# Response phase of a two-block image kernel: the last eleven strips of the second product rotate over three pairs of PSUM banks, the output and residual rings grow by one, and the scale is placed ahead of the add

## The reference

```python
y = depthwise_conv_7x7(x) + dw_b            # 8 x 48 x 112 x 112
y = layernorm over channels (y) * ln_g + ln_b
y = gelu(y @ w1.T + b1)                     # 192 features per pixel
gx = sqrt(sum over the image's pixels of y**2)        # one value per image and feature
nx = gx / (mean over features of gx + 1e-6)
y = grn_g * (y * nx) + grn_b + y
y = y @ w2.T + b2                           # back to 48 channels
return x + y
```

## Time and profile before

| what | value |
|---|---|
| median of 3 runs | 1980.95 us (1978.91 to 1982.73) |
| span of the profiled execution | 1974.3 us, 90330 instructions |
| its own time with what lies around the span | not given; the median run is 6.65 us above this span |
| busy, share of the span | PE 1764.7 us (89%), ACT 1540.4 (78%), DVE 1361.2 (69%), POOL 1171.4 (59%) |
| mean granted TensorE clock | 0.956 of 2.4 GHz |
| response phase | about 1610 to 1974 us of the span |

### The profile page before, as it was taken

The page is one execution under the profiler, slowest core; times in us unless marked ns, Lnnn a source line. Parts: engine busy times, 40 slices in busy tenths (PEclk is TensorE's granted clock), DMA queues, the critical chain, the costliest instruction groups (busy, mean ns, idle before and its releaser), DMA issues. The chain is left out here.

```text
span 1974.3 us, 90330 instructions
## 1 busy us (share of the span) xinstructions
PE 1764.7 (89%) x38186; PEld 1091.3 (55%) x38186; DVE 1361.2 (69%) x2016; ACT 1540.4 (78%) x2904; POOL 1171.4 (59%) x1048
## 2 busy tenths in 40 slices
PE   4999999999999999999999999985999958999994
PEld 2666656565666556565666656541699943333331
DVE  7776767676776667676776767543777757888872
ACT  3788888888888888888888888865666639988880
POOL 5677777777787777878787777742355530221222
PEclk9999999999999999999999999995899975999998
DMA  3343554444443444344444444322478758999983
GB/s 111 101 100 101 143 130 112 101 115 99 110 105 102 102 102 114 99 113 103 108 107 102 106 102 105 77 55 65 133 216 216 216 117 171 264 260 244 248 226 110
DMA packets 233227, 262.26 MB, mean 133 GB/s; under 512 B 167078, under 2 KB 179910, under 8 KB 232710
## 3 DMA queue, kind: packets, MB, share of 16 engines
q1 hardware_dynamic: 217478, 217.50, 45.0%
q0 software_dynamic: 15360, 39.08, 6.6%
HBM read 160.82 MB, written 80.88 MB: 122 GB/s over the span
## 5 line engine op out<-in xcount | busy, mean ns | idle before, releaser
L416 POOL TENSOR_TENSOR shift<-const_b,qmax 113x588 bf16<-113x588 bf16 x256 | 299.3, 1169 | 224.8 <-DVE qmax L511 223.2
L563 DVE TENSOR_TENSOR x<-ps_m,x 112x392 f32<-112x392 f32 x128 | 66.5, 562 | 267.0 <-PE ps_m L1028 267.0
L511 DVE TENSOR_REDUCE qmax<-ps_s 113x12 f32<-113x588 f32 x256 | 194.7, 761 | 65.2 <-PE ps_s L907 65.1
L1481 POOL DMA_DIRECT2D out_rolled<-r_OUT x128 | 63.8, 503 | 284.5 <-DVE r_OUT L1581 284.5
L716 ACT ACTIVATE P<-ps_t 113x588 f32<-113x588 f32 x256 | 171.9, 672 | 52.9 <-PE ps_t L959 52.2
L748 ACT ACTIVATE G<-ps_m 128x392 f32<-128x392 f32 x384 | 178.1, 499 | 43.1 <-PE ps_m L1009 43.0
L503 DVE TENSOR_TENSOR Ul<-Uf 113x784 bf16<-113x784 f32 x192 | 206.1, 1100 | 0.0
L1333 PE MATMUL conv_ps<-xin,band_now 64*64 64x448 bf16 x2688 | 202.7, 364 | 2.2 <-DVE x_low L1228 2.2
L406 POOL TENSOR_TENSOR xhl<-xh 113x784 bf16<-113x784 f32 x64 | 202.3, 3161 | 2.2 <-DVE xh L551 2.2
L709 ACT COPY Uf<-ps_m 113x392 f32<-113x392 f32 x384 | 172.6, 485 | 31.4 <-PE ps_m L874 23.2
L1333 PE MATMUL conv_ps<-x_low,band_now 64*64 64x448 bf16 x1344 | 176.5, 351 | 0.0
(11 more groups left out here) (239 smaller groups left out, 5201.1 us busy)
## 6 DMA issues: line engine op xcount, KB each, us to landing
xin<-rows_scratch SPq DMA_DIRECT2D x96, 236.0 KB, 3.7
XT<-x_tokens SPq DMA_DIRECT2D x64, 294.0 KB, 3.2
X<-x_windows SPq DMA_DIRECT2D x128, 147.0 KB, 3.3
RS<-rs_scratch SPq DMA_DIRECT2D x128, 147.0 KB, 3.3
XR<-x_windows SPq DMA_DIRECT2D x128, 147.0 KB, 3.2
x_scratch<-x SPq DMA_DIRECT2D x128, 147.0 KB, 3.4
y_scratch<-y POOLq DMA_DIRECT2D x96, 196.0 KB, 2.8
r_RS<-rs_scratch SPq DMA_DIRECT2D x128, 147.0 KB, 4.7
```

What stands on the lines that cost most here:

```text
L416: nc.gpsimd.tensor_tensor(shift[:, j % 2], e, m, ALU.mult).then_inc(S["md"], 1)
L511: nc.vector.tensor_reduce(qmax[:, j % 2, :].rearrange("p (b n) -> p b n", b=2), ps_s[0:R, :, 0:2 * HQ].rearrange("p b (n t) -> p b n t", t ...
```

## The change

All of it is in `response_phase`.

```diff
-        XRING = 3
+        XRING = 4
+        ORING = 3
-        OUT = sb("r_OUT", [ROWB + C, 2, STRIP])
+        OUT = sb("r_OUT", [ROWB + C, ORING, STRIP])
-        stored = [sem(f"r_stored{r}") for r in range(2)]
+        stored = [sem(f"r_stored{r}") for r in range(ORING)]
+        late = (ps_o, ps_f[0], ps_f[1])
+
+        def out_banks(s):
+            return late[max(0, s.raw - (N - LAG)) % len(late)]
...
                     nc.vector.scalar_tensor_tensor(
-                        out=halves(OUT[:, s.slot(2), :]), in0=ps_o[0:n, :, 0:HALF], scalar=out_b[:, 0:1],
+                        out=halves(OUT[:, s.slot(ORING), :]), in0=out_banks(s)[0:n, :, 0:HALF], scalar=out_b[:, 0:1],
...
                 add_up(s.at(-STRIPS))
+                respond(s.at(-STRIPS - 2))
                 finish(s.at(-LAG))
-                respond(s.at(-STRIPS - 2))
                 normalise(nx2)
...
-                    wait(pe, S["out_made"], s.n)
+                    turn = s.n - (N - LAG)
+                    if turn <= 0:
+                        wait(pe, S["out_made"], s.n)
+                    elif turn < len(late):
+                        wait(pe, S["ge"], 3 * N)
+                    else:
+                        wait(pe, S["out_made"], s.n - len(late) + 1)
+                    out = out_banks(s)
...
-                            mm(ps_o[lo:lo + ROWB, b, 0:HALF], w2s_own[:, p, :], G[:, slot, g, cols],
+                            mm(out[lo:lo + ROWB, b, 0:HALF], w2s_own[:, p, :], G[:, slot, g, cols],
```

More of the change, by code:

```diff
@@ L1481, in store @@
                         pool.dma_start(by_strip[1][s.n // STRIPS, s.n % STRIPS, g],
-                                       OUT[ROWB * g:ROWB * g + C, s.slot(2), :]).then_inc(stored[s.slot(2)], 16)
+                                       OUT[ROWB * g:ROWB * g + C, s.slot(ORING), :]).then_inc(stored[s.slot(ORING)], 16)
             def step(s):
@@ L1487, in _ @@
             steps(step, N + LAG)
-            for r in range(2):
-                pool.wait_ge(stored[r], 32 * (N // 2))
+            for r in range(ORING):
+                pool.wait_ge(stored[r], 32 * len(range(r, N, ORING)))
         @block.vector
@@ L1578, in finish @@
                     wait(dve, x2_loaded[s.slot(XRING)], 32 * (s.raw // XRING + 1))
-                    wait(dve, stored[s.slot(2)], 32 * s.turn(2))
+                    wait(dve, stored[s.slot(ORING)], 32 * (s.raw // ORING))
                     wait(dve, S["f2"], s.n + 1)
                     nc.vector.scalar_tensor_tensor(
-                        out=halves(OUT[:, s.slot(2), :]), in0=ps_o[0:n, :, 0:HALF], scalar=out_b[:, 0:1],
+                        out=halves(OUT[:, s.slot(ORING), :]), in0=out_banks(s)[0:n, :, 0:HALF], scalar=out_b[:, 0:1],
                         in1=halves(X2[:, s.slot(XRING), :]), op0=ALU.add, op1=ALU.add).then_inc(S["out_made"], 1)
@@ L1727, in fc2 @@
                             lo, at = F2 * half, ROWB * (half ^ b)
-                            ins = mm(ps_o[at:at + ROWB, b, 0:HALF], w2s_both[lo:lo + F2, p, :],
+                            ins = mm(out[at:at + ROWB, b, 0:HALF], w2s_both[lo:lo + F2, p, :],
                                      G[lo:lo + F2, slot, 2, cols], start=False, stop=True)
```

## The result

The changed kernel took 1973.69 us in the median of 9 runs (1962.39 to 1977.35), the kernel before, beside it on the same chip, 1982.73 (1977.88 to 1990.52). The ratio of the two is 0.9929, 95% interval 0.9907 to 0.9951: 0.7% faster, which is 14.1 us of 1980.95. The ratio of the two medians is 0.9954, just outside that interval: the runs of either kernel spread over 13 to 15 us, and the median of nine fell in the lower half of that spread before (mean 1983.82) and in the upper half after (mean 1970.58). The median of the change, 1973.69, is above the forecast range of 1962.0 to 1972.0; the ratio carried to 1980.95, the time from which the prediction started, gives 1966.9, inside it.

What follows compares the result with a forecast made beforehand. In the last strips TensorE and VectorE take turns on one pair of banks, 3.62 us a strip. Terms -12.1 + 0.25 - 2.0 = -13.9 on 1980.95 give about 1967.0 us, range 1962.0 to 1972.0.

Steps and rivals of the forecast that it cites:

- the main term: Last eleven strips of the response phase: strip 63 starts at 1944.30 instead of 1956.41, -12.1 us.
- The last eleven strips: Strips 53 to 63: `fc2` back to back at 2.36 us a strip instead of 3.62, -12.1 us (bounds -12.7 and -11.8).
- Weights ready in time: Last image: scaled weights end at 1927.15, strip 56 can start at 1927.78, 0.6 us to spare.
- What must keep up: Last strips: VectorE, POOL, loads, DMA and output ring all keep up with a beat of 2.36 us.
- the rival: Last strips: landing of stores in the output ring sets the beat, 2.91 us, time 1971.4; chance 0.12.
- Start of the phase: Set-up: the longer clear of `X2` starts the chain of weights later, +0.25 us (bounds 0 and 0.68).
- Earlier images: Six earlier images: no wait for scaled weights, fourth `X2` slot eases SP's queue; -2.0 us, range -4.7 to +2.8.
- The output ring: Rival, last strips: slow landings of stores set the beat at 2.91 us, time 1971.4; chance 0.12.
- The earlier stage gets worse: Rival, earlier images: early `X2` loads delay `Y`, +2.8 and the -2.0 lost, 1971.8 us; chance 0.08.
- Low clock: Rival, last eleven strips: clock falls, `fc2` takes 4.33 us, time 1989.7; chance 0.03.
- The beat stays: Rival, last strips: an overlooked wait keeps 3.62 us, only the head's 3.3 is won, 1975.9 us; chance 0.03.

Runs made afterwards that it cites:

- the smallest version: Against the changed kernel: two pairs of banks instead of three, three slots of `X2` instead of four; 1969.25 us, ratio 0.9911; again 1972.40 us, ratio 0.9936.

## Why the prediction was right

The ratio 0.9929 on the 1980.95 that the prediction started from gives 1966.9 us, against 1967.0. That they agree to 0.1 us is luck: the interval of the ratio, 0.9907 to 0.9951, is a gain of 9.7 to 18.4 us. The sum inside the phase, -13.69 against -13.9, is close by luck as well: the last eleven strips gave 0.74 us more than forecast, the earlier images 0.95 less. What was not luck is the main term, right to 6% and by the mechanism forecast; the term of the earlier images was not shown.

**The last eleven strips** (-12.1, measured -12.84). Strip by strip: to strip 54 3.32 us (3.39 by the prediction's times), to 55 2.82 (2.90), to 56 2.29 (2.36), and seven beats in 16.01 (16.52). The mechanism is the predicted one in each step; what was mis-sized is the beat. It came out at the lower bound, 2.29: an `fc2` behind an `fc2` starts 0.07 us before the end of its last matmul, just as the next instruction did in the earlier trace rows, while the busy time of 2.36 runs to that end. The step from a group to the next instruction of another kind was the better row. The two earlier steps came out 0.07 and 0.08 shorter in the same way.

**Weights ready in time**: 0.57 us to spare, 0.6 predicted. The two edits are not independent, though: with the old order 2.30 us of the banks' gain would have been lost, with the old beat the order gives 0.90.

**What must keep up.** VectorE and POOL did. The DMA share was 0.66 over the stretch. The forecast of 0.8 to 0.9, the traffic of a beat with loads and stores over the shorter beat, holds for the three beats in which seven loads of `X2` and seven stores were issued, and neither ahead of them, at the start of the fast beat (0.67 from 1937.50 to 1944.40, six of each), nor after them, where one load was left. Windows of the three beats and of the three after:

```profile
1944.40:1951.20 6.80, 6.80 (x52) 2.07 (x48) 3.10 (x3) 0.00 (x0) 2.93 (x7) 1.00 0.84 263
1951.20:1958.10 6.90, 6.90 (x52) 2.08 (x48) 3.10 (x3) 0.00 (x0) 3.02 (x7) 1.00 0.62 178
```

DMA issues from 1933 to 1962 (count, KB each, median us to landing):

```profile
out_rolled<-r_OUT POOLq DMA_DIRECT2D x22, 147.0 KB, 2.9
r_X<-x_scratch SPq DMA_DIRECT2D x14, 147.0 KB, 3.0
```

The output ring made no sum wait in the two profiles of the change, but it has little to spare. At the beat of 2.29 three slots hold a landing of 3 x 2.29 - 1.82 = 5.05 us, not the 5.26 worked out for 2.36, and 0.07 less with the hand-over from the landing (1955.53 + 4.00 in the chain of the banks alone) to the sum (1959.60); the longest in these strips was 4.6 in both profiles of the change and 5.0 in the second one of the smallest version, where one sum waited for a store and came 0.07 us late. Timeline of DVE, that version:

```profile
1949.31 1.03 DVE L1587 SCALAR_TENSOR_TENSOR r_OUT<-r_ps_o,r_out_b,r_X 112x784 f32<-112x784 f32 x1 [1.25 <-PE r_ps_o L1741]
1951.67 1.03 DVE L1587 SCALAR_TENSOR_TENSOR r_OUT<-r_ps_f,r_out_b,r_X 112x784 f32<-112x784 f32 x1 [1.33 <-DMA out_rolled<-r_OUT]
```

By the same sum two slots hold a landing of 2 x 2.29 - 1.82 = 2.76 us, and the landings of 4.00 there made VectorE wait. Had the change left the ring at two, the rival would have come true, at a price of 3.0 us.

The Trainium skill, page "DMA: Bandwidth & Descriptors", section "Anatomy of one DMA", by which the prediction had an estimate of 2.35 us, would have let even two slots do; the measured 4.00 decides.

**Start of the phase** (+0.25, measured +0.19). Timeline of POOL and DVE after, against the earlier trace rows:

```profile
1623.99 2.70 POOL L1481 MEMSET r_X<- 112x3136 f32 x1
```

```profile
1626.56 0.06 DVE L1508 MEMSET r_eps<- 128x1 f32 x1
1626.73 0.24 DVE L1511 TENSOR_SCALAR r_aug<-pack_r 48x48 f32<-48x48 f32 x1
```

The clear ends at 1626.69 and VectorE goes on at 1626.73; its own clears ended at 1626.62 and hid the rest of the longer clear, as expected.

**Earlier images** (-2.0, measured -1.05, not shown). The wait for the scaled weights, 1.9 us, is gone in all nine profiles with the new order and there (1.9 to 2.2) in all three with the old one. But the stretch of strips 0 to 52 took 241.46 to 245.28 us with the new order, 243.33 in the mean, and 241.67 to 245.09 with the old, 243.88. The difference of 0.5 is far inside that spread. Two other things vary beside it: TensorE's waits for totals and sums add up to 2.8 in the profile of before and to 4.2 to 8.1 with the new order, but to 6.3 and 8.0 in the other two with the old; and the granted clock of the stretch lay between 0.96 and 0.99. So the term should have been the bounds without a value, 0 to -4.7 or +2.8. A loss through `Y` is not borne out either: its wait was 13.8 to 18.5 us in every kernel but the one profile that I had, with three slots or four.

**The rivals.** *The output ring* did not bind in the two profiles of the change and did with two slots. *The earlier stage gets worse*: not seen, as above. *Low clock*: 1.00 in the last strips of the change, as in the earlier trace rows. The Trainium skill, page "TensorE: Matmul & The Clock Gate", section "A second HAM failure mode: psum-queue depth-cycling", has the clock swing in a rotation through PSUM banks that leaves TensorE brief idle gaps; here hardly a gap was left (busy for 26.75 of 27.30 us), and no run with a rotation, of two pairs or three, shows a swing: the step is 2.29 us in all eight. *The beat stays*: only without the banks.

## What to carry to other kernels

Two engines that take turns on one buffer, each idle for a third of the beat or more, want a second buffer; here a third added nothing, the consumer's work (1.03 us) being shorter than the producer's (2.29). Every ring further down the line has then to be sized anew for the shorter beat: slots x beat must hold the sum, the issue and the landing, and the landing to put in is the slow one (4.0 to 5.0 us here), not the median (2.9). And where the runs of a kernel spread by 15 us, compare between landmarks inside the phase that changed: a term of 12 us was read there to 0.1.

## What the runs showed that was not expected

The unchanged part of the program makes most of the difference between runs: in the twelve profiles here the response phase begins between 1610.16 and 1626.38 us, with the same instructions ahead of it, while strips 0 to 52 lie within 3.8 us. And the same wait of 2.24 us of TensorE left the clock at 1.00 in two kernels and was followed by 0.57 for one strip in a third, at a price of 1.56 us (5.17 less 3.61).
